# A gather that accumulates: keys and values added onto edge features and zeros in the attention stage of a graph network

## The chip, the cores and the metric

One Trainium2 chip, one of its cores. The metric is the device time of one execution in microseconds, median of three runs. An engine is TensorE (PE, its weight loads PEld), VectorE (DVE), ScalarE (ACT), GpSimd (POOL) or SyncE (SP); transfers run on 16 DMA engines.

## What is computed

2500 nodes with 256 features each, 40,000 edges sorted by destination. The program runs a relational graph layer, a mixture of six experts, an edge attention layer with a feed-forward part, and a mixture of eight experts. The change is in the attention:

```python
ep = ef @ We + be                                     # 40000 x 32, from 64 edge features
scores = einsum("ehd,ehd->eh", q[dst], k[src] + ep[:, None, :]) * scale
scores = scores * ew[:, None]
m = segment_max(scores, dst);  ex = exp(scores - m[dst]);  s = segment_sum(ex, dst)
out = segment_sum((ex / s[dst])[:, :, None] * v[src], dst)   # 8 heads of 32
```

Each edge needs the row of its source node in a table of keys and values (512 numbers, 2 KB), and the same 32 edge features are added to each of the 8 heads of the key.

## The kernel before, in words

The stages follow each other: loading, tables, sums and experts of the first half, then `stage_attention` (line 1749), whose first instructions run at 817 us of the profile. Behind it stand code paths for unsorted edges that don't run here.

`stage_attention` handles the edges in 79 groups of 4 tiles of 128 edges (TP = 4, NG = 79; 314 tiles in all, as the last group has two). Every engine has its own list of pieces, made by `order1` (line 1735) from two tables: SLOT1 says at which place of a slot a group's piece stands, so that piece `("add", -0.280)` of group 10 stands at 9.720, and BLOCK1 does the same for the ten blocks of 256 nodes of feed-forward and expert work that begin once their groups are done. Sorting by place gives the order in which an engine issues. The pieces of a group `i`:

- GpSimd gathers four times 128 rows of 2 KB from `table_kv` in HBM into the ring `kv` of 9 groups (line 1890, `att_kv<-table_kv,g_srcI`; RINGC = 9). Groups 0 to 2 wait for nothing, 3 to 8 for the add of three groups before, later ones until the sums of the group that had the place are done (`summed`, line 1887). After a group's first gather stands the join of an earlier group (line 1882), an accumulating DMA of 1 KB to `table_o`, whose waits hold up the three gathers behind it.
- SyncE loads the edge features (`eft`, line 2459, two buffers), the queries and selection matrices (lines 2452, 2453, 2470), and stores sums.
- TensorE makes the features in `psE` (line 2284, `features`, piece "feat") and the queries in `psQ` (line 2276), later sums weighted values (line 2301, `sums`).
- ScalarE copies `psE` to the buffer `epb`, 128 columns (line 2188, `features`), scales scores (line 2195), copies half of each sum (`odd`, line 2227).
- VectorE adds `epb` to the keys, each feature row repeated for 8 heads (line 1910, `add`), multiplies by the queries (line 1915), reduces to scores (line 1921), and 7 slots later multiplies the values by the weights (line 1997, `weigh`). A softmax over 4 groups at a time runs in between.

In the ring a tile has 8 spare columns, then 256 for keys and 256 for values. Semaphores tie the engines: `ep_made` (features in PSUM), `ep_ready` (in `epb`), `added`, `product`, `summed`.

## Time and profile before

| | us |
|---|---|
| three runs | 1721.68, 1724.7, 1732.46 |
| median of the runs | 1724.7 |
| span of the profiled execution, first to last instruction | 1668.6 |
| first gather of the attention stage issued | 817.55 |
| last one issued | 1485.6 |

No device time of its own is given for the profiled execution; the span lies 56.1 us below the median of the runs. Busy over the span: TensorE 1495.7 us (90%), VectorE 1028.6 (62%), ScalarE 615.6 (37%), GpSimd 781.2 (47%). The stage's end is what is late: the table of stretches tells which engine is full where. TensorE's clock has two levels, 1.2 and 2.4 GHz; the granted clock is given as a share of the higher one, so a stretch at 0.5 ran at the lower level, one at 0.6 mostly so.

### The profile page before, as it was taken

Reading aid. Unit: us, or ns where it says so; the run is one execution under the profiler, and the core shown is the slowest. Engines: PE = TensorE matmul, PEld = TensorE weight load, DVE = VectorE, ACT = ScalarE, POOL = GpSimd, SP = SyncE. Lnnn points to the kernel's source line nnn. Section 1 sums busy time; section 2 is a strip of 40 time slices with the busy share of each in tenths; the row PEclk is TensorE's granted clock in tenths of the full one; section 3 lists DMA queues with packets and bytes.
Section 4 is the critical chain, followed back from the end, with each engine's and each line's share of the span. In section 5 each row is a group of like instructions: output and inputs, shape, how many; then the busy total and the mean of one; then the engine's idle time right before and its main releaser. Section 6 shows DMA issues by size and latency. Waiting matters only on the chain. (4 is left out here: it accounts for less than half of the span.)

```text
span 1668.6 us, 23723 instructions
## 1 busy us (share of the span) xinstructions
PE 1495.7 (90%) x6795; PEld 1005.9 (60%) x6795; DVE 1028.6 (62%) x2542; ACT 615.6 (37%) x1534; POOL 781.2 (47%) x738
## 2 busy tenths in 40 slices
PE   4999788999999999998356799999999999999996
PEld 2554314665666777777233467767766767767785
DVE  6543244345445555545388789898898888896432
ACT  3121002333234343443022355554555445555341
POOL 1100277646755777600378666574746556540000
PEclk9999857999999999999556699999999999999997
DMA  8448456546766566631487885665757565641100
GB/s 258 164 161 261 142 151 172 154 115 191 213 175 180 166 190 178 164 94 47 137 252 216 267 253 165 193 180 167 208 152 212 143 196 169 179 122 39 29 7 9
DMA packets 191573, 270.07 MB, mean 162 GB/s; under 512 B 28295, under 2 KB 156035, under 8 KB 188867
## 3 DMA queue, kind: packets, MB, share of 16 engines
q1 hardware_dynamic: 148419, 144.77, 27.7%
q0 software_dynamic: 43008, 123.61, 26.8%
q8 instruction: 60, 0.98, 0.2%
q14 instruction: 86, 0.70, 0.1%
HBM read 196.22 MB, written 72.06 MB: 161 GB/s over the span
## 5 line engine op out<-in xcount | busy, mean ns | idle before, releaser
L1890 POOL DMA_INDIRECT att_kv<-table_kv,g_srcI x314 | 368.5, 1174 | 246.4 <-issue 180.4
L1149 POOL DMA_INDIRECT ex_hg<-table_h,z_idx x314 | 316.7, 1008 | 150.2 <-issue 84.9
L2441 PE MATMUL att_psR<-g_mw,att_h 128*128 128x256 f32 x640 | 163.9, 403 | 1.0 <-ACT att_h L2259 1.0
L2414 PE MATMUL att_psR<-att_t,g_mw 128*128 128x256 f32 (+1 forms) x640 | 154.8, 387 | 0.1
L1466 PE MATMUL ex_psG<-ex_hg,ex_oh 128*42 128x256 f32 x628 | 134.6, 427 | 13.3 <-DMA ex_hg<-table_h,z_idx 7.2
L751 PE MATMUL tab_psH<-e_u,tab_xT 128*128 128x512 f32 x320 | 142.6, 598 | 4.3 <-DVE e_u L532 4.3
L2441 PEld LDWEIGHTS att_psR<-g_mw,att_h 128*128 128x128 f32 x640 | 124.7, 200 | 23.0 <-ACT att_h L2259 4.0
L1387 ACT ACTIVATE ex_h<-ex_psH,g_cols 128x256 f32<-128x256 f32 (+1 forms) x240 | 97.3, 464 | 93.8 <-PE ex_psH L1488 93.1
L2414 PEld LDWEIGHTS att_psR<-att_t,g_mw 128*128 128x128 f32 x640 | 121.2, 199 | 16.6 <-issue 2.6
L1882 POOL DMA_DIRECT2D table_o<-att_part x59 | 54.2, 919 | 161.9 <-DMA table_o<-att_part 90.5
L2301 PE MATMUL att_psG<-att_kv,att_oh 128*42 128x264 f32 x628 | 109.5, 431 | 13.7 <-DVE att_kv L1997 13.3
L1910 DVE TENSOR_TENSOR att_kv<-att_kv,att_epb 128x1024 f32<-128x1024 f32 x79 | 96.4, 1220 | 39.9 <-DMA att_kv<-table_kv,g_srcI 32.9
L1501 PE MATMUL ex_psC<-e_experts,ex_h 128*128 128x256 f32 x480 | 114.0, 384 | 0.0
L1488 PE MATMUL ex_psH<-ex_xT,e_experts 128*128 128x256 f32 (+1 forms) x480 | 113.8, 380 | 0.1
L1215 DVE TENSOR_TENSOR ex_part<-ex_psG,ex_odd 42x256 f32<-42x256 f32 x79 | 32.5, 411 | 130.6 <-ACT ex_odd L1400 130.4
L1488 PE MATMUL ex_psH<-ex_h,e_experts 128*128 128x256 f32 (+1 forms) x480 | 111.6, 377 | 0.0
L2259 ACT ACTIVATE att_h<-att_psR,g_cols 128x256 f32<-128x256 f32 (+1 forms) x160 | 66.2, 464 | 116.8 <-PE att_psR L2414 116.4
L2105 DVE SCALAR_TENSOR_TENSOR att_acc<-att_psR,att_gate,att_acc 128x256 f32<-128x256 f32 x160 | 69.5, 475 | 59.8 <-PE att_psR L2441 59.8
L751 PEld LDWEIGHTS tab_psH<-e_u,tab_xT 128*128 128x128 f32 x320 | 60.8, 192 | 74.3 <-issue 71.0
L1501 PEld LDWEIGHTS ex_psC<-e_experts,ex_h 128*128 128x128 f32 x480 | 88.9, 190 | 19.6 <-issue 7.2
L1997 DVE TENSOR_TENSOR att_kv<-att_kv,att_p 128x1024 f32<-128x1024 f32 x79 | 95.5, 1209 | 7.0 <-ACT att_p L2212 6.9
L1488 PEld LDWEIGHTS ex_psH<-ex_xT,e_experts 128*128 128x128 f32 x480 | 87.7, 190 | 17.6 <-issue 7.7
(308 smaller groups left out, 2465.1 us busy)
## 6 DMA issues: line engine op xcount, KB each, us to landing
table_h<-tab_hs SPq DMA_DIRECT2D x20, 1024.0 KB, 4.0
att_eft<-in_eft SPq DMA_DIRECT2D x158, 64.0 KB
ex_db<-table_dst SPq DMA_DIRECT2D x79, 126.0 KB
table_ohT<-ex_ohT SPq DMA_DIRECT2D x79, 126.0 KB
att_ohT<-table_ohT SPq DMA_DIRECT2D x79, 126.0 KB
table_oh<-ex_oh SPq DMA_DIRECT2D x79, 84.0 KB, 2.3
att_oh<-table_oh SPq DMA_DIRECT2D x79, 84.0 KB, 4.0
table_kv<-ex_qkv SPq DMA_DIRECT2D x10, 512.0 KB, 4.8
```

Of the source, the lines that this page charges most:

```text
L751: ins = nc.tensor.matmul(psH[:, c % 4, :], xT[:, b % 2, k, q * P:(q + 1) * P], Wr[:, k, j * 512:(j + 1) * 512], start=(k == 0), stop=(k == ...
L1149: nc.gpsimd.indirect_dma_start(hg[:, t % RING0, :], None, d.h[:, :], bass.IndirectOffsetOnAxis(ap=g.idx0[:, t:t + 1], axis=0)).then_inc(go ...
L1387: nc.scalar.activation((h1 if what == "A" else h2)[:, e % 2, o, 0:used(b)], psH[:, n % 3, o * BLK0:o * BLK0 + used(b)], ACT.Relu, bias=vec ...
L1466: ins = nc.tensor.matmul(psG[at:at + WG, 0:D], oh[:, i % 3, t % TP, :], hg[:, t % RING0, :], start=(t <= second), stop=(t >= tiles(i)[-1] ...
L1488: ins = nc.tensor.matmul(psH[:, n % 3, o * BLK0:o * BLK0 + w_], w[:, e, k, o * P:(o + 1) * P], x[:, k, 0:w_], start=(k == 0), stop=(k == D ...
L1501: ins = nc.tensor.matmul(psC[:, e % 2 * BT0 + q, :], h2[:, e % 2, k, q * P:(q + 1) * P], g.w3[:, e, k, :], start=(k == 0), stop=(k == DK - 1))
L1890: nc.gpsimd.indirect_dma_start(kv[:, t % (RINGC * TP), H:H + 2 * D], None, d.kv[:, :], bass.IndirectOffsetOnAxis(ap=g.srcI[:, t:t + 1], ax ...
L1910: nc.vector.tensor_tensor(k, k, epb[:, i % 2, :, :].unsqueeze(2).to_broadcast([P, TP, H, DH]), ALU.add).then_inc(s.added, 1)
L1997: nc.vector.tensor_tensor(kv[:, b:b + TP, 0:H * VW].rearrange("p t (a c) -> p t a c", c=VW)[:, :, :, 0:DH], kv[:, b:b + TP, H + D:H + 2 * ...
L2301: ins = nc.tensor.matmul(psG[at:at + WG, 0:H * VW], oh[:, i % 3, t % TP, :], kv[:, t % (RINGC * TP), 0:H * VW], start=(t <= second), stop= ...
L2414: ins = nc.tensor.matmul(out[:, c * CB:c * CB + used(b)], g.mw1[:, e, k, c * P:(c + 1) * P], t3[:, k, 0:used(b)], start=(k == 0), stop=(k ...
L2441: ins = nc.tensor.matmul(out[:, q * D:(q + 1) * D], h1[:, n % 3, k, q * P:(q + 1) * P], g.mw2[:, e, k, :], start=(k == 0), stop=(k == DK - 1))
```

## The change

The buffer `epb` and VectorE's add are gone. ScalarE now writes into the ring before the gather comes: zeros into the 256 value columns of the four tiles, and the features, repeated for 8 heads, into the 256 key columns (`fill`, two copies of 128x1024). The gather is issued with `compute_op=ALU.add`, so that the DMA adds each row to what lies there. GpSimd waits for both copies of a group before its first gather; the ring's wait for `summed` has moved into `fill`, and groups 3 to 8 wait for `product` of three groups before. Features run further ahead: TensorE makes those of group `b + 3` at place 0.600 of slot `b` in place of group `b + 1` at -0.236, SyncE loads them up to group `b + 4`, and ScalarE fills group `b + 2` at -0.100. Features of a group stand tile by tile in `psE` by another output pattern.

```diff
 SLOT1 = {
-    "PE": (("sums", -0.271), ("feat", -0.236), ("cols", -0.027), ...
+    "PE": (("sums", -0.271), ("cols", -0.027), ... ("turnR", 0.580), ("feat", 0.600), ...
...
-                        if i >= RINGC and t % TP == 0:
-                            pool.wait_ge(s.summed, i - RINGC + 1)
-                        elif i >= 3 and t % TP == 0:
-                            pool.wait_ge(s.added, i - 2)
+                        if t % TP == 0:
+                            pool.wait_ge(s.keys_filled, i + 1)
+                            pool.wait_ge(s.values_cleared, i + 1)
+                            if 3 <= i < RINGC:
+                                pool.wait_ge(s.product, i - 2)
                         nc.gpsimd.indirect_dma_start(kv[:, t % (RINGC * TP), H:H + 2 * D], None, d.kv[:, :],
-                                                     bass.IndirectOffsetOnAxis(ap=g.srcI[:, t:t + 1], axis=0)).then_inc(kv_got[i % RINGC], 16)
+                                                     bass.IndirectOffsetOnAxis(ap=g.srcI[:, t:t + 1], axis=0), compute_op=ALU.add).then_inc(kv_got[i % RINGC], 16)
...
-                def add(i):
+                def multiply(i):
                     dve.wait_ge(kv_got[i % RINGC], 64 * (i // RINGC) + 16 * len(tiles(i)))
-                    dve.wait_ge(s.ep_ready, i + 1)
-                    k = keys(i).rearrange("p t (a c) -> p t a c", c=DH)
-                    nc.vector.tensor_tensor(k, k, epb[:, i % 2, :, :].unsqueeze(2).to_broadcast([P, TP, H, DH]), ALU.add).then_inc(s.added, 1)
-
-                def multiply(i):
-                    dve.wait_ge(s.added, i + 1)
                     dve.wait_ge(s.q_ready, i + 1)
                     nc.vector.tensor_tensor(keys(i), keys(i), psQ[:, :, :], ALU.mult).then_inc(s.product, 1)
...
-                def features(i):
+                def fill(i):
+                    b = i % RINGC * TP
+                    if i >= RINGC:
+                        act.wait_ge(s.summed, i - RINGC + 1)
+                    if i == 0:
+                        act.wait_ge(s.zero_made, 1)
+                    nc.scalar.copy(kv[:, b:b + TP, H + D:H + 2 * D], zero[:, 0:1].unsqueeze(2).to_broadcast([P, TP, D])).then_inc(s.values_cleared, 1)
                     act.wait_ge(s.ep_made, i + 1)
-                    if i >= 2:
-                        act.wait_ge(s.added, i - 1)
-                    nc.scalar.copy(epb[:, i % 2, :, :].rearrange("p (a t) c -> p t a c", a=2),
-                                   psE[:, 0:P].rearrange("p (t a c) -> p t a c", a=2, c=DH)).then_inc(s.ep_ready, 1)
+                    nc.scalar.copy(kv[:, b:b + TP, H:H + D].rearrange("p t (a c) -> p t a c", c=DH),
+                                   psE[:, 0:P].rearrange("p (t c) -> p t c", c=DH).unsqueeze(2).to_broadcast([P, TP, H, DH])).then_inc(s.keys_filled, 1)
...
-                        features(0)
+                        fill(0)
+                        fill(1)
...
-                        queries(0)
-                        features(0)
+                        for i in range(3):
+                            features(i)
+                        queries(0)
...
+                        load_features(2, features)
+                        load_features(3, features)
```

In the changed kernel the multiply is line 1910, the reduction 1916, the gather 1891, ScalarE's two copies 2182 (zeros) and 2184 (features), the copy of half a sum 2224, the scaling of scores 2191, TensorE's features 2280 and queries 2271.

VectorE, one slot early in the stage, before (1997 is `weigh`, 2009 the sum of two halves):

```order
L1910 TENSOR_TENSOR att_kv<-att_kv,att_epb 128x4x256
L2009 TENSOR_TENSOR att_part<-att_psG,att_odd 42x264
L1997 TENSOR_TENSOR att_kv<-att_kv,att_p 128x4x8x32
L1915 TENSOR_TENSOR att_kv<-att_kv,att_psQ 128x4x256
L1921 TENSOR_REDUCE att_S<-att_kv 128x32
```

and now:

```order
L2004 TENSOR_TENSOR att_part<-att_psG,att_odd 42x264
L1992 TENSOR_TENSOR att_kv<-att_kv,att_p 128x4x8x32
L1910 TENSOR_TENSOR att_kv<-att_kv,att_psQ 128x4x256
L1916 TENSOR_REDUCE att_S<-att_kv 128x32
L2004 TENSOR_TENSOR att_part<-att_psG,att_odd 42x264
```

The row of the add is gone, the others follow as they did, with the multiply directly behind `weigh`.

ScalarE, the same place of the program, before (2219 copies the softmax weights beside the values):

```order
L2227 COPY att_odd<-att_psG 42x264
L2219 COPY att_kv<-att_p 128x4x8
L2188 COPY att_epb<-att_psE 128x2x2x32
L2195 ACTIVATE att_S<-att_S,g_ews 128x8 x4
L2227 COPY att_odd<-att_psG 42x264
```

and now:

```order
L2224 COPY att_odd<-att_psG 42x264
L2182 COPY att_kv<-att_zero 128x4x256
L2184 COPY att_kv<-att_psE 128x4x256
L2216 COPY att_kv<-att_p 128x4x8
L2191 ACTIVATE att_S<-att_S,g_ews 128x8 x4
```

One copy of 128 columns, behind the weights, has become two of 1024, in front of them and behind `odd`.

SyncE at the start of the stage, behind the features, selection and queries of group 0 and the features of group 1, before:

```order
L2452 DMA att_ohT<-table_ohT 126x512
L2453 ISA
L2453 DMA att_qw<-table_q 126x256
L2465 DMA att_mk<-table_masks 128x386 x2
L2470 DMA att_oh<-table_oh 128x168 x3
L2459 DMA att_eft<-in_eft 64x256 x2
```

and now:

```order
L2447 DMA att_ohT<-table_ohT 126x512
L2448 ISA
L2448 DMA att_qw<-table_q 126x256
L2454 DMA att_eft<-in_eft 64x256 x4
L2460 DMA att_mk<-table_masks 128x386 x2
L2465 DMA att_oh<-table_oh 128x168 x3
```

Two more groups of features are loaded ahead of the masks and windows.

## Rows read from the trace of the kernel before

**Rows 1.** Which engines are busy in which stretch: busy us (instructions), granted clock, DMA share

```profile
817.00:860.00 43.00, 16.57 (x67) 11.90 (x68) 24.43 (x32) 7.41 (x29) 33.00 (x32) 0.50 0.87 257
...
1500.00:1668.60 168.60, 144.20 (x682) 117.32 (x680) 70.67 (x212) 61.14 (x122) 3.90 (x5) 0.93 0.07 21
817.00:960.00 143.00, 86.90 (x344) 49.06 (x346) 107.78 (x156) 37.43 (x143) 108.03 (x95) 0.59 0.83 245
960.00:1500.00 540.00, 520.18 (x2743) 379.79 (x2740) 470.67 (x950) 273.87 (x735) 310.73 (x274) 0.98 0.63 181
```

**Rows 2.** The page, chain that ended last, by engine

```profile
PE 27%; DVE 8%; issue 5%; POOL 4%; DMA 3%; ACT 1%; SPq 1%; POOLq 0%; DVEq 0%
```

**Rows 3.** TensorE's waits, 960 to 1500 us: waiting, releaser, total us, times, longest

```profile
PE att_psR L2428 <- DVE att_gate L967: 8.5, 7, 1.3
PE att_psR L2433 <- ACT att_gateT L2266: 3.8, 7, 0.5
PE att_psT L2340 <- DVE att_fnew L1951: 2.5, 5, 0.8
PE att_psE L2284 <- ACT att_epb L2188: 2.1, 6, 0.4
PE att_psR L2314 <- DVE att_n L2025: 1.7, 1, 1.7
```

**Rows 4.** Waits of all engines, 817 to 960 us

```profile
DVE att_kv L1910 <- DMA att_kv<-table_kv,g_srcI: 17.4, 10, 2.7
```

**Rows 5.** DMA queues and one issue row, 817 to 960 us: packets, MB, share

```profile
q0 software_dynamic: 6957, 21.90, 51.7%
q1 hardware_dynamic: 16732, 12.95, 30.3%
...
att_kv<-table_kv,g_srcI POOLq DMA_INDIRECT x86, 4.6
```

**Rows 6.** DMA queues, 960 to 1500 us

```profile
q0 software_dynamic: 19891, 60.50, 39.7%
q1 hardware_dynamic: 47496, 36.42, 22.9%
```

**Rows 7.** The page, costliest groups: busy us, mean ns of one, idle before

```profile
L1882 POOL DMA_DIRECT2D table_o<-att_part x59 | 54.2, 919 | 161.9 <-DMA table_o<-att_part 90.5
...
L1910 DVE TENSOR_TENSOR att_kv<-att_kv,att_epb 128x1024 f32<-128x1024 f32 x79 | 96.4, 1220 | 39.9 <-DMA att_kv<-table_kv,g_srcI 32.9
```

**Rows 8.** Timeline of the stage's start: start us, us, engine, line

```profile
817.55 1.08 POOL L1890 DMA_INDIRECT att_kv<-table_kv,g_srcI  x1 [93.13 <-issue]
818.27 1.16 SPq L2459 DMA_DIRECT2D att_eft<-in_eft  x2
...
820.65 0.36 SPq L2453 DMA_DIRECT2D att_qw<-table_q  x1
...
822.72 0.95 POOL L1890 DMA_INDIRECT att_kv<-table_kv,g_srcI  x1 [0.30 <-issue]
...
825.32 1.01 PE L2276 MATMUL att_psQ<-att_qw,att_ohT 126*128 126x256 bf16 x4 [18.42 <-DMA att_qw<-table_q]
...
826.12 0.95 PE L2284 MATMUL att_psE<-g_we,att_eft 128*128 128x64 f32 x4
...
828.77 1.22 DVE L1915 TENSOR_TENSOR att_kv<-att_kv,att_psQ 128x1024 f32<-128x1024 f32 x1
```

**Rows 9.** The reduction of line 1921, one per group, 860 to 960 us

```profile
860.00:960.00 100.00, 16.60 (x15) 0.63 0.81 240
```

**Rows 10.** DMA queues around one 1 MB store, 68.8 to 74.5 us

```profile
q1 hardware_dynamic: 144, 1.05, 44.5%
```

**Rows 11.** ScalarE's groups by shape, 817 to 1500 us

```profile
L2188 ACT COPY att_epb<-att_psE 128x128 f32<-128x128 f32 x79 | 20.7, 262 | 39.3 <-PE att_psE L2284 38.7
...
L2254 ACT COPY att_t<-att_psR 128x512 f32<-128x512 f32 x7 | 4.1, 586 | 6.5 <-PE att_psR L2314 6.5
```

**Rows 12.** Timeline, one expert layer's matmuls

```profile
1207.31 1.89 PE L2414 MATMUL att_psR<-att_t,g_mw 128*128 128x256 f32 x8
```

More of the change, by code:

```diff
@@ L2109, in program @@
                     if not redo:
+                        nc.vector.memset(zero[:, :], 0.0).then_inc(s.zero_made, 1)
                         nc.vector.memset(ends[:, :, :], -FAR)
@@ L2231, in program @@
                                 scale(i)
-                        if what == "feat":
-                            i, j = b, b - LAG
-                            if i + 1 < NG:
-                                features(i + 1)
+                        if what == "fill" and b + 2 < NG:
+                            fill(b + 2)
                         if what == "att":
@@ L2345, in program @@
                                 queries(i + 1)
[L2346 to L2349 removed]
+                        if what == "feat" and b + 3 < NG:
+                            features(b + 3)
                         if what == "ends":
@@ L2513, in steps @@
                                     load_windows(j + 3)
-                        if what == "loadE" and b + INS < NG:
-                            load_features(b + INS, features)
+                        if what == "loadE" and b + 4 < NG:
+                            load_features(b + 4, features)
                         if what == "loadQ" and b + INS < NG:
```

25 lines of the change are left out of this document (9 added, 16 removed).

## The prediction

> **What bounds the kernel now.** I read the view by stretches first. The attention stage (817 to 1668.6 us) falls into three parts [rows 1]. From 817 to 960 us the matmul engine is busy 87 of 143 us at a granted clock of 0.59, so it is mostly at the 1.2 GHz level and not the limit; VectorE is busy 108 us, GpSimd 108 us and the DMA engines 83%. Three resources are close to each other there. From 960 to 1500 us TensorE is busy 520 of 540 us at clock 0.98: it is the bound, VectorE has 69 us free, DMA is at 63%. From 1500 us no gather is left, DMA is at 7%, and the rest is expert matmuls.
>
> The chain that ended last agrees: TensorE has 27% of the span in it, VectorE 8%, GpSimd's gather 4%, DMA 3% [rows 2]. The waits say what TensorE lacks in the middle part: its five named waits make 18.6 us in 540, of which 12.7 us are for VectorE (8.5, 2.5 and 1.7) [rows 3]. In the first part VectorE's add waited for the gather ten times, 17.4 us in all [rows 4]: gathers already arrive late there.
>
> Last, the DMA queues. q0, the queue that GpSimd feeds, carries practically only this gather. It took 51.7% of the 16 engines' time from 817 to 960 us, q1, all that SyncE issues, 30.3% [rows 5]; from 960 to 1500 us 39.7% and 22.9% [rows 6]. So one gather of 256 KB costs the engines 73.9 us / 86 = 0.86 us in the first part, and over the stage (73.9 + 214.4) / 314 = 0.92 us.
>
> **The change part by part.**
>
> *The add.* 79 instructions of 1220 ns, 96.4 us of VectorE [rows 7]. About 20 of them lie before 960 us (86 gathers at 4 a group [rows 5], which lead the add by one or two groups), 24 us. The other 59 (72 us) lie beside TensorE's matmuls; at most the 12.7 us that TensorE waited for VectorE can come back. In the first part at most 24 us can, and only if gathers keep up. They hardly can: a group is 4 gathers of 0.95 us [rows 8] and a join of 0.92 us [rows 7], each with 0.30 us before it, so 4 × 1.25 + 1.22 = 6.22 us of GpSimd, against a pace of 100 us / 15 groups = 6.67 us [rows 9]. Over the 20 groups that caps the gain at 20 × 0.45 = 9 us. What is late next is the gather itself.
>
> *The add inside the gather.* The sum now needs the destination's old 256 KB beside the source's: 82 MB more to read from SBUF. No row shows a large accumulating transfer (the joins move 1 KB), so I bound it. From below: the second read is hidden and costs nothing, 0.92 us stays. From above: it costs as much again as the gather, 1.84 us. The nearest row of a read out of SBUF is a 1 MB store of the tables stage: 44.5% of 5.7 us is 2.54 us of engine time for 1.05 MB, 2.42 us per MB [rows 10]. I take that, put behind the gather's own time, since it is the only measured price of that leg: 0.262 MB × 2.42 = 0.63 us more, 1.55 us a gather, 1.69 times as much.
>
> First part: 73.9 + 21.9 MB × 2.42 (53.0) + 43.3 for q1 = 170.2 us of engine time for what took 143 us. The highest mean share that the stretches show is 0.87, while engines still waited for other things [rows 1]; pressed harder I take 0.90. 170.2 / 0.90 = 189 us: **+46 us**. VectorE's 24 us lie within these waits, so they give nothing.
>
> Middle part: 214.4 + 60.5 MB × 2.42 (146.4) + 123.7 = 484.5 us, 0.90 of 540. That is just at the edge, **0 us**; at 0.87 it would be 557, +17. The at most 12.7 us of TensorE's waits for VectorE go into the waits for gathers.
>
> *The order of the start.* Before, the first gather was issued at 817.55 us, beside the loads, and the first multiply began at 828.77 [rows 8]. Now the gather must wait for features: eft's load (issued 818.27 to 819.43), landing some 4.6 us later as qw's did (820.65 to 825.3), 0.95 us of features matmul, 1.0 us of ScalarE copy, four gathers of 1.25 us, a landing of 4.6 us [rows 5]: 819.4 + 4.6 + 0.95 + 1.0 + 5 + 4.6 = 835.6, seven late. Later groups are fed by the same queues that are the limit of this part, so it is not caught up, save for perhaps 1 us of idle time before the third group: **+6 us**.
>
> *ScalarE's two copies.* From its copies of 128x128 (262 ns) and 128x512 (586 ns) [rows 11] a column costs 0.84 ns, so 1024 columns take 1.02 us. Two of them replace one of 262 ns: +1.78 us a group, 79 groups, 140 us. ScalarE was busy 274 of 540 us in the middle part and goes to 379 [rows 1], behind which nothing is queued that TensorE lacks at once: expert layers are issued two ahead, and one layer's matmuls take 1.9 us [rows 12], nearly as long as both copies. I cost it at nothing; without that cover a copy pair would hold TensorE perhaps 1 us in 59 groups, 59 us.
>
> *The rest.* The gather's wait moves from `summed` to a fill that itself waits for `summed`, so group i is issued some 2 us later than before, and used 0.6 of a slot later (multiply in place of add, 0.6 × 8.5 us): even. Behind GpSimd's wait stands the join, for which SyncE's next wide store waits at every fourth group. TensorE's features matmuls keep their count and only move. SyncE's two feature loads go three groups ahead, no bytes added. The memset of `zero` is one of 128x1. All 0; if features came late they would now hold a gather, not an add, and the ring of two feature buffers is unchanged, so I allow 5 us for it.
>
> Sum: 46 + 0 + 6 = +52 us on the profiled execution. Its span is 1668.6 us; the median of the three runs is 1724.7, so 56 us lie around the span, untouched. 1724.7 + 52 = **1777 us**. With the share at 0.87 the same sum gives 1724.7 + 53 + 17 + 6 = 1801.
>
> **The rivals.**
>
> *R1, the second read costs as much as the first* (1.84 us a gather). First part 147.8 + 43.3 = 191.1, at 0.90 212 us, +69; middle 428.8 + 123.7 = 552.5, at 0.90 614 us, +74; start +6: 1874 us. At a share of 1.0 it would be 48 + 13 + 6, 1792. For it: both reads pass the same engines, which show no spare rate above 0.9. Against: SBUF reads went at 2.42 us per MB, not 3.5. The Trainium skill, "Collectives: The Full Stack", section "The bandwidth ceiling: the fold count and why AG ≠ RS ≠ AR", says that an add in the DMA path costs nothing by itself but needs two source reads on one ring, so it runs at about half the rate of a copy; by its ratio of 1.93 the sum would lie just under R1. No large accumulate in this trace confirms it.
>
> *R2, both legs run at the store's rate* (2 × 0.63 = 1.27 us, as if part of the gather's time were waiting that the second leg fills). First part 2 × 53.0 + 43.3 = 149.3, at 0.90 166 us, +23; middle 2 × 146.4 + 123.7 = 416.5 of 540, no bound; start +6, minus half of the 12.7 us of waits: 1748 us. For it: the store shows that the engines can pass 413 GB/s (1 / 2.42), where the gather reaches 21.9 MB / 73.9 us = 296. Against: no row shows that one read fills the other's waiting.
>
> *R3, the other side: the second read is hidden.* The DMA share stays as it is and VectorE's time comes back: −9 in the first part (GpSimd's floor), −13 in the middle, +6 for the start: 1709 us. If GpSimd's gathers also shorten, and the start is caught up, all of −24 − 13: 1688. It decides as soon as an accumulating gather costs under about 1.0 us of engine time: then 86 × 1.0 + 43.3 = 129 us still fit into 143 at 0.90. For it: GpSimd's join, which accumulates too, is no dearer to issue than a plain gather [rows 7, 8]. Against: two reads must be paid somewhere.
>
> *R4, the change takes the work from VectorE but puts it in TensorE's way through ScalarE*, 59 us as above with a free accumulate: 1709 + 59 = 1768. Against: TensorE waited for ScalarE 5.9 us in 540 [rows 3].
>
> **How the numbers follow.** Forecast 0.35, R1 0.17, R2 0.15, R3 0.28, R4 0.05. R1 spreads from 1792 to 1874 and R3 from 1688 to about 1720; the range leaves out the outer end of each, a tenth of the chance on either side: 1705 to 1860. What a measurement of this kernel tells from no change is about 1%, 17 us, so the bounds are 1707 and 1742. Slower: the forecast but for 0.01, R1, R4 and 0.08 of R2, 0.64. Within 1%: 0.11 of R3 (1709 lies 2 us inside), 0.07 of R2 and that 0.01, 0.19. Faster: the better part of R3, 0.17.
>
> **What would show it.** Right: q0's share per gather rises to about 1.55 us of engine time; the DMA share from 817 to 960 us at 0.9; multiply waits for the gather in nearly every early group; the last gather is issued some 50 us later than 1485; the stretch after the last gather is unchanged. VectorE loses 96 us of busy time and gains as much idle. The start is read from the first multiply, 7 us later. ScalarE's copies at 1.0 us each. Wrong: q0 per gather at or under 1.0 us (R3), at 1.84 us (R1), GpSimd's own instruction grown well beyond 0.95 us (a cost that I put at nothing: each 0.25 us of it adds 1 us a group where GpSimd is at its floor), or TensorE idle behind ScalarE (R4).

## The result, and the profile after

On the chip that timed the change, the kernel before takes 1723.7 us (median of 4 runs, 1721.7 to 1732.5) and the changed one 1777.1 us (4 runs, 1773.3 to 1779.0): ratio 1.0324, 95% interval 1.0274 to 1.0373, 53 us slower. The forecast said 1777.0. The number was met by luck. The sections below show that its account was met only in part: one term was sized about right for a mostly wrong reason, one was missing, and on other chips the same change costs 77 us and not 53.

The first thing to read is the span. The profiled execution of after took 1776.4 us with a span of 1774.6, so less than 2 us lie around the span, not 56. The profile of before [rows 1] has a span of 1668.6 us, and the kernel before took 1666 to 1670 us (medians) on the three chips of most experiments below; it took 1723.7 us where the change was timed, and 1722.8 on the chip of c13. So "span against median" compared two chips. I call the chip that timed the change the timing chip. In after's profile the unchanged stages ahead of the attention end at 856 us and not at 817.

**The stage by stretches.** After: the first 144 us, the middle, and what follows the last gather (columns: window, its length, busy us and instructions of TensorE, its loads, VectorE, ScalarE, GpSimd, granted clock, DMA share, GB/s).

```profile
856.00:1000.00 144.00, 69.75 (x269) 38.26 (x269) 65.75 (x98) 58.45 (x132) 117.35 (x77) 0.50 0.99 190
1000.00:1500.00 500.00, 447.35 (x2291) 325.74 (x2291) 349.12 (x768) 315.77 (x671) 376.33 (x242) 0.94 0.93 176
1596.00:1774.60 178.60, 154.21 (x741) 123.61 (x739) 80.19 (x229) 66.82 (x137) 7.20 (x8) 0.94 0.10 25
```

Against [rows 1]: in the first stretch the DMA engines are at 0.99 where they were at 0.83, GpSimd is busy 117 us for 77 instructions where it needed 108 for 95, and TensorE and VectorE do far less. In the middle TensorE is busy 89% of the time, not 96%, and its granted clock is 0.94, not 0.98; that window of after still holds some of the early groups. The stretch after the last gather is no longer than before (178.6 us; from 1485.6 to 1668.6 it was 183).

**The gather.** Page of after, costliest groups (busy us, mean ns of one, idle before and what ended it), and the two DMA queues from 857 to 1600 us:

```profile
L1891 POOL DMA_INDIRECT att_kv<-table_kv,g_srcI x314 | 523.6, 1667 | 243.2 <-ACT att_kv L2184 153.9
...
L1910 DVE TENSOR_TENSOR att_kv<-att_kv,att_psQ 128x1024 f32<-128x1024 f32 x79 | 95.7, 1211 | 74.3 <-DMA att_kv<-table_kv,g_srcI 71.5
...
L1992 DVE TENSOR_TENSOR att_kv<-att_kv,att_p 128x1024 f32<-128x1024 f32 x79 | 95.7, 1211 | 48.3 <-ACT att_p L2209 47.0
...
L1882 POOL DMA_DIRECT2D table_o<-att_part x59 | 75.5, 1280 | 80.3 <-DMA table_o<-att_part 58.3
```

```profile
q0 software_dynamic: 46809, 82.27, 70.5%
q1 hardware_dynamic: 63872, 49.12, 23.1%
```

q0 took 0.705 of 743 us for 314 gathers, 1.67 us of engine time each; it was 0.92 [rows 5, 6], so 1.82 times as much. It makes 149 packets a gather, where before it made 85 (26848 packets for 314 [rows 5, 6]). The instruction on GpSimd grew as well, from typically 0.95 us [rows 8] (median 974 ns) to 1.54 (median 1543), and the join from 919 ns [rows 7] to 1280. The mean of a gather lies higher in both kernels, 1667 ns here and 1174 in the page of before:

```profile
L1890 POOL DMA_INDIRECT att_kv<-table_kv,g_srcI x314 | 368.5, 1174 | 246.4 <-issue 180.4
```

The forecast had GpSimd's room from the 0.95 us. VectorE no longer has the add (96.4 us) and waits for gathers 71.5 us instead of 32.9. The wait of line 1992 is new in size: VectorE waits 47.0 us for the exponentials that ScalarE makes.

**ScalarE and the chain.** ScalarE's two fills by shape, and the chain that ended last:

```profile
L2182 ACT COPY att_kv<-att_zero 128x1024 f32<-128x1024 f32 x79 | 82.3, 1041 | 10.4 <-DVE att_zero L2105 10.4
L2184 ACT COPY att_kv<-att_psE 128x1024 f32<-128x1024 f32 x79 | 79.9, 1012 | 11.8 <-PE att_psE L2280 10.0
```

```profile
PE 21%; ACT 9%; DVE 6%; issue 5%; POOL 5%; DMA 4%; SPq 1%; POOLq 0%; DVEq 0%
```

A fill takes 1.0 us, as worked out. ScalarE had 1% of the chain [rows 2] and has 9%.

**The start.** Timeline of after (start us, us, engine, line; in brackets the idle time before and what ended it):

```profile
856.07 1.16 SPq L2454 DMA_DIRECT2D att_eft<-in_eft  x2
...
858.95 1.09 PE L2280 MATMUL att_psE<-g_we,att_eft 128*128 128x64 f32 x4 [14.26 <-DMA att_eft<-in_eft]
...
860.08 1.01 ACT L2184 COPY att_kv<-att_psE 128x1024 f32<-128x1024 f32 x1 [0.95 <-PE att_psE L2280]
861.36 1.64 POOL L1891 DMA_INDIRECT att_kv<-table_kv,g_srcI  x1 [99.20 <-ACT att_kv L2184]
...
863.30 1.56 POOL L1891 DMA_INDIRECT att_kv<-table_kv,g_srcI  x1 [0.30 <-issue]
...
874.19 1.22 DVE L1910 TENSOR_TENSOR att_kv<-att_kv,att_psQ 128x1024 f32<-128x1024 f32 x1 [15.43 <-DMA att_kv<-table_kv,g_srcI]
```

Features, fill, first gather, and four gathers before the first multiply can start: 18.1 us from the load to the multiply. The kernel before needed 10.5 [rows 8], and 12.6 in its second profile (c1).

### The profile page after: what moved, and what is told of

Its sections match the earlier page's. It is cut to its first block, busy times and chain, and to the rows that moved or that the text cites. A ratio compares the mean times of both kernels' runs of the same rounds, so it can differ in the third digit from the quotient of the medians.

```text
span 1774.6 us, 23647 instructions
## 1 busy us (share of the span) xinstructions
PE 1513.0 (85%) x6795; PEld 1017.4 (57%) x6795; DVE 943.9 (53%) x2464; ACT 747.6 (42%) x1613; POOL 931.5 (52%) x738
## 4 chain that ended last, share of the span: by engine, by line
PE 21%; ACT 9%; DVE 6%; issue 5%; POOL 5%; DMA 4%; SPq 1%; POOLq 0%; DVEq 0%
PE att_psR L2436 7%; POOL att_kv L1891 4%; PE att_psR L2409 3%; PE att_psR L2385 3%; PE att_psG L2297 2%; PE att_psR L2394 2%; ACT att_kv L2184 2%; ACT att_kv L2182 2%; DVE att_kv L1910 2%; ACT L2254 2%; DMA table_o<-att_part 1%; ACT att_h L2254 1%; DMA att_kv<-table_kv,g_srcI 1%; DMA att_eft<-in_eft 1%; ACT L2207 1%
## 5 line engine op out<-in xcount | busy, mean ns | idle before, releaser
L1891 POOL DMA_INDIRECT att_kv<-table_kv,g_srcI x314 | 523.6, 1667 | 243.2 <-ACT att_kv L2184 153.9
L2436 PE MATMUL att_psR<-g_mw,att_h 128*128 128x256 f32 x640 | 167.6, 409 | 11.2 <-ACT att_h L2254 11.2
L1910 DVE TENSOR_TENSOR att_kv<-att_kv,att_psQ 128x1024 f32<-128x1024 f32 x79 | 95.7, 1211 | 74.3 <-DMA att_kv<-table_kv,g_srcI 71.5
L1992 DVE TENSOR_TENSOR att_kv<-att_kv,att_p 128x1024 f32<-128x1024 f32 x79 | 95.7, 1211 | 48.3 <-ACT att_p L2209 47.0
L1882 POOL DMA_DIRECT2D table_o<-att_part x59 | 75.5, 1280 | 80.3 <-DMA table_o<-att_part 58.3
L1400 ACT COPY ex_odd<-ex_psG 42x256 f32<-42x256 f32 x79 | 29.1, 368 | 199.5 <-PE ex_psG L1466 102.9
L2254 ACT ACTIVATE att_h<-att_psR,g_cols 128x256 f32<-128x256 f32 (+1 forms) x160 | 66.0, 463 | 102.0 <-PE att_psR L2409 100.8
L1466 PEld LDWEIGHTS ex_psG<-ex_hg,ex_oh 128*42 128x42 f32 x628 | 43.8, 126 | 104.0 <-issue 86.3
```

The lines of the kernel that those rows point to most:

```text
L1466: ins = nc.tensor.matmul(psG[at:at + WG, 0:D], oh[:, i % 3, t % TP, :], hg[:, t % RING0, :], start=(t <= second), stop=(t >= tiles(i)[-1] ...
L1891: nc.gpsimd.indirect_dma_start(kv[:, t % (RINGC * TP), H:H + 2 * D], None, d.kv[:, :], bass.IndirectOffsetOnAxis(ap=g.srcI[:, t:t + 1], ax ...
L1910: nc.vector.tensor_tensor(keys(i), keys(i), psQ[:, :, :], ALU.mult).then_inc(s.product, 1)
L2254: nc.scalar.activation(h1[:, n % 3, k, 0:used(b)], psR[:, bank["A", b, e], k * CB:k * CB + used(b)], ACT.Gelu, bias=vec(g, "mb1", 2 * e + ...
L2436: ins = nc.tensor.matmul(out[:, q * D:(q + 1) * D], h1[:, n % 3, k, q * P:(q + 1) * P], g.mw2[:, e, k, :], start=(k == 0), stop=(k == DK - 1))
```

## The experiments

Each was run beside the kernel before on the same chip, and the ratio is to that. They ran in four sets, each on a chip of its own: c1 to c4 (before: 1667.9 us), c5 to c8 (1669.7), c9, c10 and c12 (1666.3), and c13 on a chip where before takes 1722.8. Beside the times stands what separated the theories best: when VectorE's reduction, one per group, starts for the 1st, 21st, 31st, 71st and 79th time in each profile's timeline, and what is left of the span then. In after these reductions stand at 875.45 and, for example,

```profile
1141.16 1.21 DVE L1916 TENSOR_REDUCE att_S<-att_kv 128x32 f32<-128x1024 f32 x1
...
1536.67 1.21 DVE L1916 TENSOR_REDUCE att_S<-att_kv 128x32 f32<-128x1024 f32 x1
```

for the 31st and the 71st group: 40 groups in 395.5 us.

| kernel | median us | ratio (95%) | 1st starts at | 1 to 21 | 21 to 31 | 31 to 71 | 71 to 79 | rest |
|---|---|---|---|---|---|---|---|---|
| before | 1668 | 1 | 830.0 | 136.6 | 92.0 | 372.9 | 73.4 | 163.7 |
| c1 before, once more | 1665.5 | 1.000 (0.997 to 1.003) | 834.5 | 132.7 | 91.2 | 372.1 | 73.4 | 163.8 |
| c6 plain gather, narrow fills | 1654.6 | 0.992 (0.989 to 0.995) | 833.0 | 125.2 | 93.0 | 363.3 | 72.8 | 163.8 |
| c12 the same, ScalarE kept busy | 1685.4 | 1.012 (1.009 to 1.015) | 830.0 | 130.3 | 97.2 | 388.3 | 73.7 | 163.7 |
| c2 plain gather, wide fills | 1701.2 | 1.020 (1.014 to 1.025) | 831.8 | 133.3 | 98.4 | 395.5 | 76.0 | 163.9 |
| c3 c2 and GpSimd work | 1719.3 | 1.032 (1.027 to 1.037) | 830.7 | 149.8 | 97.0 | 395.6 | 75.9 | 162.0 |
| c7 c2 and DMA traffic | 1730.5 | 1.037 (1.033 to 1.041) | 832.5 | 155.3 | 105.9 | 395.4 | 76.0 | 163.4 |
| c8 every second accumulates | 1716.7 | 1.029 (1.025 to 1.033) | 833.5 | 148.0 | 97.6 | 395.4 | 75.9 | 163.5 |
| c4 accumulates 1 KB rows | 1734.4 | 1.042 (1.036 to 1.047) | 834.0 | 164.1 | 96.9 | 395.5 | 76.0 | 162.0 |
| c9 accumulates, narrow fills | 1710.3 | 1.027 (1.023 to 1.031) | 836.0 | 170.2 | 95.9 | 365.2 | 71.1 | 164.0 |
| c10 fills behind the weights | 1756.6 | 1.053 (1.049 to 1.056) | 840.4 | 168.8 | 103.5 | 405.6 | 74.8 | 163.7 |
| c5 the changed kernel | 1746.6 | 1.047 (1.043 to 1.050) | 835.7 | 171.7 | 100.3 | 395.5 | 76.0 | 165.2 |
| after: the changed kernel, timing chip | 1777.1 | 1.032 (1.027 to 1.037) | 875.5 | 168.4 | 97.3 | 395.5 | 75.9 | 162.0 |
| c13 zeros by VectorE | 1769.4 | 1.028 (1.024 to 1.032) | 873.5 | 169.2 | 100.8 | 385.9 | 72.7 | 163.7 |

One profile stands behind each row. Two profiles of the same kernel show how far a column can be trusted: before and c1 differ by 4.4 us at the start, 3.9 in groups 1 to 21 and at most 0.9 in the others; c5 and after by 3.3, 3.0 and 3.2 us in groups 1 to 21, 21 to 31 and the rest, and by 0.1 or less in 31 to 71 and 71 to 79.

Two columns carry the finding. "1 to 21" follows the gather (c2, c3, c8, c4 and c5 have the same ScalarE), and "31 to 71" does not: it is 395.5 us with any gather as long as ScalarE's fills are wide, and 363 to 365 with narrow ones, whether the gather accumulates or not.

### c1: the kernel before, once more

> The kernel before, profiled once more. The two profiles differ before the attention stage too: its first gather goes out at 817 us in the profile of before and its first feature load at 856 us in that of the changed kernel, in code that the change does not touch. Theory A (the profile of before caught a shorter execution than its timed ones): this profile has a span near 1720 us and a first gather 30 to 50 us later than 817. Rival (the early stages really run faster before): span near 1670 again, first gather near 817, and the timed runs have 50 us outside the span.

1665.5 us (10 runs), ratio 0.9998 (0.9969 to 1.0027); its profiled execution took 1669.0 us with a span of 1667.5. Theory A falls: the span is near 1670 again, as its rival had it, with the first gather at 819.9 us. But nothing large lies around the span either. The 56 us were a difference between two chips (or two occasions; no run separates these).

### c2: the changed kernel with a plain gather

```diff
-  bass.IndirectOffsetOnAxis(ap=g.srcI[:, t:t + 1], axis=0), compute_op=ALU.add)
+  bass.IndirectOffsetOnAxis(ap=g.srcI[:, t:t + 1], axis=0))
```

The gather overwrites the features, so they are not added: this part of the computation is left out.

> The changed kernel with the accumulate taken out of the gather and all else kept (ScalarE's two copies, the waits, the order; the keys then lack the edge features). If the accumulate is what costs (my step 2), the time falls to that of before or somewhat under it: 1705 to 1735 us, a gather at 0.95 us on GpSimd and 0.9 us of DMA engine time. If ScalarE's copies or the later start cost (R4, step 3), it stays over 1750 us.

1701.2 us: 33 us over the kernel before with no accumulate at all and no add on VectorE. The bounds of c2 to c4 were written for a chip where before takes 1723.7 us; taken as differences, c2 should have come out between 19 us faster and 11 slower if only the accumulate cost. 33 slower is past the 26 from which it was to be ScalarE's copies or the later start. It falls in no term of the forecast. Page of c2:

```profile
PE 26%; ACT 12%; DVE 8%; issue 3%; DMA 2%; POOL 1%; SPq 0%; DVEq 0%; POOLq 0%
...
L1891 POOL DMA_INDIRECT att_kv<-table_kv,g_srcI x314 | 325.9, 1038 | 386.7 <-ACT att_kv L2184 306.5
...
L1992 DVE TENSOR_TENSOR att_kv<-att_kv,att_p 128x1024 f32<-128x1024 f32 x79 | 95.7, 1211 | 51.3 <-ACT att_p L2209 51.3
```

The gathers are early (GpSimd waits for ScalarE, 306.5 us), and ScalarE has 12% of the chain. The wait of line 1992 for the exponentials was 6.9 us in the kernel before.

### c3: GpSimd's time alone

```diff
+  if t > 0:
+      pool.wait_ge(s.idled, t)
+  nc.gpsimd.memset(idle[:, :], 0.0).then_inc(s.idled, 1)
```

behind each plain gather, a memset of 128x512. Here, too, the features are not added.

> The plain gather again, with a memset of 128x512 on GpSimd behind each gather, which puts back about the 0.6 us by which the accumulating gather is longer on GpSimd (1.54 in place of 0.95 us), with no added DMA traffic. Theory G (GpSimd's time to issue is the new bound: 4 x 1.84 + 1.6 = 9.0 us a group): at least two thirds of the loss comes back, 1755 to 1785 us. Theory D (the DMA engines' doubled reads are the bound, my forecast): under 1740 us.

1719.3 us, 18 us over c2. GpSimd's timeline:

```profile
859.18 0.95 POOL L1893 DMA_INDIRECT att_kv<-table_kv,g_srcI  x1 [0.17 <-issue]
860.14 0.54 POOL L1897 MEMSET att_idle<- 128x512 f32 x1
860.84 0.95 POOL L1893 DMA_INDIRECT att_kv<-table_kv,g_srcI  x1 [0.17 <-issue]
```

A gather with its memset takes 1.66 us, a group 6.64. From the 1st to the 11th reduction, where joins have hardly begun, a group took 6.76 us. GpSimd's time alone sets the pace there. But c3 gives less than the accumulate's issue: a plain gather with its gap is 0.95 + 0.30 = 1.25 us, this pair 1.66, the accumulating one 1.54 + 0.30 = 1.84. It put back 0.41 us of 0.59, as the gap shrank to 0.17, so its 18 us are only a part of what GpSimd's longer instruction costs. The two thirds that theory G wanted, 30 of 45 us, did not come back; by this run alone neither theory holds.

### c4: accumulate, half the bytes

```diff
-  nc.gpsimd.indirect_dma_start(kv[:, t % (RINGC * TP), H:H + 2 * D], None, d.kv[:, :],
+  nc.gpsimd.indirect_dma_start(kv[:, t % (RINGC * TP), H:H + D], None, d.x2[:, :],
```

Rows of 1 KB from another table are added onto the keys; neither keys nor values of the source node are gathered.

> The changed kernel with half as many bytes in each accumulating gather: 1 KB rows of another table of as many rows, added onto the keys only; the values stay zero. GpSimd's instruction and count stay. Theory G: the instruction stays at about 1.54 us and the time within 15 us of 1777. Theory D: DMA engine time per gather falls to 0.55 of 1.67 us, and the time to 1725 us or below.

1734.4 us, 12 under c5 and 33 over c2: theory G was right in both its signs. The instruction is as long as with 2 KB rows (median 1544 ns). The window from 860 to 910 us lies in the first ten groups of both kernels; c4, then c5:

```profile
860.00:910.00 50.00, 24.74 (x104) 13.81 (x105) 28.91 (x48) 19.94 (x49) 42.40 (x28) 0.53 0.67 120
```

```profile
860.00:910.00 50.00, 26.23 (x108) 14.96 (x108) 27.73 (x46) 21.67 (x53) 42.23 (x28) 0.53 1.02 189
```

The engines' share is 0.67 and 1.02, GpSimd's busy time the same (42 us and 28 gaps of 0.30 us fill the 50), and the first ten groups took the same, 75.8 and 76.0 us. So there the length of GpSimd's instruction is the limit, not the engines. From the 11th to the 21st, c4 takes 88.2 us and c5 95.7: there the larger transfers add 7.5 us.

The same reading for all of groups 1 to 21, in before, c2, c4 and c5:

```profile
830.03:966.59 136.56, 90.26 (x368) 50.73 (x369) 109.99 (x158) 39.46 (x150) 103.96 (x90) 0.62 0.84 250
```

```profile
831.76:965.10 133.34, 88.54 (x364) 49.40 (x366) 87.50 (x138) 71.32 (x168) 96.02 (x92) 0.58 0.87 259
```

```profile
833.96:998.05 164.09, 89.95 (x364) 50.38 (x366) 88.08 (x138) 71.09 (x167) 139.85 (x89) 0.55 0.73 142
```

```profile
835.67:1007.34 171.67, 92.74 (x374) 52.03 (x374) 88.00 (x137) 72.66 (x170) 137.42 (x90) 0.56 1.01 197
```

With 0.30 us before each instruction GpSimd fills 131 of 137 us in the kernel before, 124 of 133 in c2, all 164 in c4 and 164 of 172 in c5. GpSimd was full in this part before the change already, at a mean gather of nearly 1.2 us, so what its instruction grows by can't hide there: from c2 to c5 its busy time grows by 41 us and the stretch by 38. c4 pays 31 of these 38 with the DMA engines at 0.73.

### c5: the changed kernel on this chip

> The changed kernel itself, as the anchor of the other runs on this chip, where the kernel before takes 1668 us and not 1723. Theory P (the change costs the same share everywhere, as it lies in the attention stage alone, and that stage is as long on both chips): the attention stage was 851 us before and 918 after, +67 us, so 1735 us, ratio 1.040; about 17 of the 56 us that the faster chip saves were saved in the stages ahead. Rival C (the change costs 3.24% wherever it runs): 1722 us.

1746.6 us, ratio 1.0465, 77 us slower. Rival C, the same 3.24% on every chip, falls (1722 us), and theory P (1735) came 12 us short. The changed kernel's attention stage is not longer on the timing chip (918.5 us there, 928 here), so it would have to be the kernel before that is slower in this stage there; no profile of it on that chip was taken.

### c6: narrow fills

```diff
-  nc.scalar.copy(kv[:, b:b + TP, H + D:H + 2 * D], zero[:, 0:1].unsqueeze(2).to_broadcast([P, TP, D]))
+  nc.scalar.copy(kv[:, b:b + TP, H + D:H + D + 8], zero[:, 0:1].unsqueeze(2).to_broadcast([P, TP, 8]))
...
-  nc.scalar.copy(kv[:, b:b + TP, H:H + D].rearrange("p t (a c) -> p t a c", c=DH),
-                 psE[:, 0:P].rearrange("p (t c) -> p t c", c=DH).unsqueeze(2).to_broadcast([P, TP, H, DH]))
+  nc.scalar.copy(kv[:, b:b + TP, H:H + DH], psE[:, 0:P].rearrange("p (t c) -> p t c", c=DH))
```

on top of c2.

> Plain gather, with the order, the waits and the late start of the change, but ScalarE writes only 8 columns of zeros and 32 columns of features a tile (two copies of 128x32 and 128x128, some 0.5 us together in place of 2.05). The features are not added: this leaves part of the computation out. With wide copies the plain gather took 1701 us, 33 over the kernel before. Theory S (ScalarE's 2.05 us a group, in front of the exponentials, the weights and half of each sum, is what costs these 33 us): at or under the kernel before, 1640 to 1665 us, VectorE's wait for the softmax weights gone (51 us with wide copies), and the difference from 1701 is the price of the width. Rival O (the late start and GpSimd's and TensorE's new waits cost it): above 1680 us. If VectorE's add was worth something, it shows here: 7 for the start is lost and up to 22 won.

1654.6 us, 47 us under c2: the width of the two copies costs more than everything else in c2. It also shows what losing VectorE's add is worth while the copies are small: 15 us. Of that 7 to 11 came in groups 1 to 21, by which profile of before one takes, and 9 to 10 in 31 to 71.

TensorE's waits from 1100 to 1500 us (total us, times, longest), c6, then c5:

```profile
PE att_psR L2422 <- DVE att_gate L967: 7.9, 6, 1.3
PE att_psR L2427 <- ACT att_gateT L2260: 3.3, 6, 0.5
```

```profile
PE att_psR L2436 <- ACT att_h L2254: 8.6, 5, 1.7
PE att_psR L2423 <- DVE att_gate L967: 6.6, 5, 1.3
PE att_psR L2428 <- ACT att_gateT L2261: 4.4, 5, 0.9
PE att_psG L2296 <- DVE att_crow L1985: 3.6, 11, 0.3
PE att_psG L2297 <- issue: 3.1, 6, 0.5
PE att_psE L2280 <- ACT att_kv L2184: 3.0, 5, 0.6
PE att_psT L2328 <- ACT att_S L2191: 2.8, 5, 0.6
```

11.2 us in 400 became 32.1, of which 18.8 are for ScalarE. The largest one is new: the second matmuls of an expert layer wait for the activation that ScalarE makes. No single wait is large; ScalarE is late for the experts, the scores and the features by turns, and for VectorE's exponentials.

The waits are not all of it. Groups 31 to 71, c6 and then c2:

```profile
1051.28:1414.58 363.30, 352.87 (x1896) 262.13 (x1895) 280.99 (x622) 195.59 (x547) 191.27 (x191) 1.00 0.64 184
```

```profile
1063.46:1458.98 395.52, 363.60 (x1896) 267.52 (x1895) 280.54 (x621) 256.13 (x546) 191.61 (x191) 0.97 0.59 169
```

Of the 32.2 us between them TensorE is idle for 21.5; in the other 10.7 it is busy, with the same 1896 matmuls, at a granted clock of 0.97 in place of 1.00. A third of what the wide fills cost here is slower matmuls.

### c7: DMA traffic alone

```diff
+  sp.dma_start(d.scratch[b * P:(b + 1) * P, :], g.f1[:, :, :].rearrange("p k c -> p (k c)")).then_inc(s.extra, 16)
```

in SyncE's program once a group, 1 MB each, on top of c2.

> Plain gather with wide fills, and SyncE stores 1 MB from SBUF to a scratch table once a group, so that the DMA engines have the reads of the old contents to do (some 2.5 us of engine time a group, as 4 x 0.63 were forecast), while GpSimd's instructions stay at 0.95 us. Features are not added: part of the computation is left out. Theory D (the engines' second read is what the accumulate costs): DMA share near 1 in the first part and near 0.9 in the middle, and 1725 to 1745 us, as the changed kernel. Theory G (GpSimd's instruction, 1.54 us in place of 0.95, is what costs; the engines had the room): 1701 to 1712 us, with VectorE's wait for the gather little above that of the plain one. The loads of SyncE stand behind the stores, which can make queries late: this would show as TensorE's wait for them and not for the gather.

1730.5 us, 29 over c2: the time that theory D named. But it can't be read as the price of the accumulate's traffic, since the edge features stand behind these stores in SyncE's queue: TensorE waited 55.0 us for them, where it waited 22.3 in c2, and VectorE's wait for the gather did not grow (20.7 us, 20.5 in c2), which is what theory G said. The run decides nothing between them.

### c8: every second gather accumulates

```diff
-  compute_op=ALU.add)
+  **(dict(compute_op=ALU.add) if t % 2 else {}))
```

> Gathers of odd tiles accumulate, those of even tiles are plain; all else is the changed kernel. Features are not added to even tiles: part of the computation is left out. GpSimd needs 2 x 1.84 + 2 x 1.25 + 1.6 = 7.8 us a group instead of 8.95 or 6.6; the engines 4 x (0.92 + 1.67) / 2 = 5.2 us a group for q0 instead of 6.7 or 3.7. Plain was 1701, the changed kernel about 1735. Theory L (each accumulate costs its share): halfway, 1718. Theory K (a resource that only binds past its edge, engines at 1.0 in the first part): nearer to plain, 1703 to 1710.

1716.7 us. Half the accumulates cost 15.6 us of the 45.4 that all of them cost (c5 less c2), a third. The expectation took 1735 for the whole; with the 1746.6 measured, halfway would be 1724. So the price is not in proportion throughout. By stretches: in the first ten groups c2, c8 and c5 take 56.8, 66.0 and 76.0 us, which is half the price for half the accumulates, as a limit by GpSimd's instruction gives; in the next ten 76.5, 82.0 and 95.7, less than a third of it.

### c9: accumulate with narrow fills

The fills of c6 from the tenth group on, and the gather of the change.

> The accumulating gather with narrow fills: full fills for the first nine groups, as the ring starts unwritten, and from then on 8 columns of zeros and 32 of features a tile, so that the gather adds onto what lies there and the output is left wrong in values. It prices the accumulate without ScalarE's load. On this chip: plain with narrow fills 1655, plain with wide fills 1701 (+46), accumulate with wide fills 1747 (+46 more). Theory I (the two costs are in different parts of the stage and add: the accumulate costs in the first part, where GpSimd is full, the wide fills in the rest): 1655 + 46 = 1701. Theory H (in the middle part ScalarE's delay now hides the accumulate; without it the pace would be 11.3 groups in 100 us, for which GpSimd needs 11.3 x (4 x 1.84 + 1.6) = 101 us and the engines 0.75 + 0.25 = 1.0, so the gather itself is the limit all through): 1710 to 1730, and VectorE waits for gathers after 1000 us, too.

1710.3 us, 56 over c6, at the lower edge of theory H. But the reason given for H is wrong: the profile's middle has no wait of VectorE for a gather from 1100 us on, and shows

```profile
1100.00:1500.00 400.00, 387.21 (x2075) 288.92 (x2074) 309.96 (x695) 213.32 (x589) 314.50 (x208) 0.99 0.97 183
```

TensorE is busy 97% at clock 0.99 with the engines at 0.97: groups 31 to 71 take 365.2 us beside 363.3 in c6. The accumulate costs 2 us there. Its price lies in groups 1 to 21, 45.0 us, with 3 each for the start and the next ten groups. (The first nine fills of c9 are wide; in the first ten groups wide fills cost 4 us between c6 and c2, so up to 4 of the 45 are theirs.)

### c10: the fills behind the weights

```diff
-  "ACT": (("odd", -0.123), ("fill", -0.100), ("exp", 0.044), ("pw", 0.245), ("scale", 1.507)),
+  "ACT": (("odd", -0.123), ("exp", 0.044), ("pw", 0.245), ("fill", 0.300), ("scale", 1.507)),
```

> The changed kernel with one number changed: ScalarE's fill stands at 0.300 of its slot, behind the exponentials and the copy of the weights, and no longer in front of them at -0.100. It computes all. Theory R (it is the place: 2.05 us in front of the exponentials hold up VectorE's weighing and TensorE's sums, 51 us of VectorE's waits): most of the 46 us comes back, 1700 to 1715, and VectorE's wait for the softmax weights falls from 47 to under 15 us. Theory T (it is the load: wherever they stand, two copies of 1 us delay something that TensorE waits for, its scores or its expert layers): 1735 to 1747, with the waits moved to the scores, half sums or expert activations.

1756.6 us, 10 slower than the change. Waits from 817 to 1600 us:

```profile
PE att_psQ L2271 <- DVE att_kv L1910: 30.4, 10, 6.4
PE att_psE L2280 <- ACT att_kv L2184: 27.8, 13, 2.9
```

VectorE's wait for the exponentials fell to 17.0 us, as theory R said, and the time did not follow: that wait was not what cost. TensorE's features now wait 27.8 us for the fill, and VectorE waits 100.1 us for gathers (73.5 in c5). Theory R falls; the waits moved as theory T said, though the time lies over its range too.

### c12: ScalarE busy, nobody waits for it

```diff
+  if i > 0:
+      act.wait_ge(s.spared, 2 * i)
+  for n in range(2):
+      nc.scalar.copy(spare[:, n, :], zero[:, 0:1].to_broadcast([P, 740])).then_inc(s.spared, 1)
```

behind the narrow fills of c6.

> Plain gather and narrow fills, and behind each pair of them ScalarE makes two copies of 740 columns (about 0.81 us each) to a buffer that nothing reads, so that ScalarE is as long at this place as with wide fills, while GpSimd and TensorE are released as early as with narrow ones. Features are not added: part of the computation is left out. Theory S (what costs is that ScalarE comes late to its next pieces): as with wide fills, 1695 to 1705. Theory W (what costs is that the gather and TensorE's next features are released late): as with narrow fills, 1655 to 1665.

1685.4 us, between both theories: 31 of the 46.6 us between c6 and c2 come from ScalarE being occupied, though nothing waits for these copies. The other 16 go with the wide fills themselves, which release GpSimd and TensorE later; that this is why they cost was not shown. (The two copies together with the narrow fills are 2.10 us a group, as long as the wide fills.)

### c13: the zeros by VectorE

```diff
+  def clear(i):
+      b = i % RINGC * TP
+      if i >= RINGC:
+          dve.wait_ge(s.summed, i - RINGC + 1)
+      nc.vector.memset(kv[:, b:b + TP, H + D:H + 2 * D], 0.0).then_inc(s.values_cleared, 1)
```

as a piece of VectorE at -0.150, in place of ScalarE's copy of line 2182.

> The changed kernel with the zeros written by VectorE (a memset of 128x1024 at place -0.150, the wait for the ring's sums moved with it) and only the features by ScalarE. It computes all. VectorE's memset of 128x256 takes 0.27 us, so one of 128x1024 takes 1.0 to 1.1 us, less than the add it lost (1.22); ScalarE is rid of 79 x 1.04 us. Theory L (each us of ScalarE in a group costs alike; the wide fills' extra 1.57 us cost 46 us, or 29 us of the total for each us): 1747 - 30 = 1717 us if VectorE has the room, and the pace in the middle part rises from 10.4 to about 11 groups in 100 us. Rival V (the time that VectorE won is spent again and delays multiply and weigh as the add did): 1730 to 1745. Neither is as fast as the kernel before, 1668, as the gather's doubled work in the first part stays.

1769.4 us where before takes 1722.8, ratio 1.0279. The change itself had 1.0324 beside the same time of before. In the stretch from 1140 to 1540 us, the change and then c13:

```profile
1140.00:1540.00 400.00, 366.48 (x1912) 269.81 (x1911) 283.51 (x623) 259.31 (x551) 302.43 (x194) 0.97 0.91 169
```

```profile
1140.00:1540.00 400.00, 377.59 (x1971) 280.49 (x1969) 324.59 (x692) 229.14 (x524) 316.14 (x199) 0.97 0.93 174
```

ScalarE is relieved, TensorE does more, and groups 31 to 71 need 385.9 instead of 395.5 us. The first part stays as it was, and the whole gain, about 8 us, is within the uncertainty of the two ratios. Theory L promised 30 us and falls; a gain of 8 is in the range that rival V gave (2 to 17 us under the change), and TensorE's waits in groups 31 to 71 of c13 bear V out:

```profile
PE att_psR L2429 <- DVE att_gate L967: 8.1, 5, 1.6
PE att_psG L2302 <- DVE att_crow L1991: 5.8, 3, 2.2
...
PE att_psR L2434 <- ACT att_gateT L2267: 2.7, 5, 0.5
```

In after TensorE waited in the same groups 18.8 us for ScalarE and 9.9 for VectorE; here it is 2.7 and 14: part of what one engine gave back the other took.

None of these beats the kernel before, except c6, which is the change without its purpose.

## Why the forecast came out, step by step

The parts can be read off the table, on chips where before takes 1668 us: c5 less before is 75.7 us of span, made of 5.7 at the start, 35.1 in groups 1 to 21, 8.3 in 21 to 31, 22.6 in 31 to 71, 2.6 to the last group and 1.5 after it. (Against c1 in place of before, the first two are 1.2 and 39.0.) The forecast had 6, 46, and 0 for the rest. By cause, the 77 us between the medians are 46.6 for the wide fills and 45.4 for the accumulate on top of them, less the 15 that c6 gains; the forecast had 0, 46 with 6 for the start, and 0.

**The start: the order right, the size within the spread.** Seven us late were forecast and +6 booked. From the first load to the first multiply the changed kernel takes 18.1 us (after; 18.0 in c5), the kernel before 10.5 and 12.6 (c1): 5.5 to 7.6 us more. What the stage loses by it is less certain, as the first reduction of c5 begins 5.7 us later than in before and 1.2 later than in c1.

**The add: right.** It was said to be worth at most 9 us at the start and 12.7 in the middle, if gathers kept up, which gave R3's 1709, a gain of 16. With the gather plain and the fills narrow (c6) the gain was 15, though GpSimd's floor, from which the 9 came, was taken with gathers of 0.95 us where their mean was nearly 1.2. In the changed kernel nothing of it is left, as forecast: VectorE's 96 us turned into waits, in after 39 us more for gathers and 40 more for the exponentials.

**The add inside the gather: the size near, the reason for the most part not.** The step priced engine time, 1.55 us a gather, and said that the engines at 0.90 would cost 46 us in the first part. Engine time is 1.67 us, between that and R1's 1.84, and the engines went to 1.0 and not 0.90. The two errors offset each other: by the same sum, 86 × 1.67 + 43.3 at a share of 1.0 is 187 us, +44. But the limit of the first part is another one, which was put at nothing: GpSimd's instruction, which grew by 0.59 us on an engine that was full already. c4 has that growth with half the bytes and keeps 33 of the 45 us that the accumulate costs (c5 over c2); c3, with 0.41 us of it and no accumulate, costs 18. The larger transfers make up the other 12 us, most of it behind the eleventh group. The forecast's own list of what would show it wrong named this growth, "a cost that I put at nothing". Its arithmetic there (0.25 us of it is 1 us a group) comes near what the chip did: 4 × 0.59 = 2.4 us a group for 20 groups is 47 us, against 38 measured between c2 and c5. The Trainium skill, "Collectives: The Full Stack", section "The bandwidth ceiling: the fold count and why AG ≠ RS ≠ AR", says of two collectives that the one with an add needs two source reads and runs at about half the rate of the one that copies, measured at a ratio of 1.93. The traces agree in size: these gathers took 1.82 times the engine time.

**The middle costs the gather nothing: right.** q0 and q1 were put at 0.90 of the engines, "just at the edge, 0 us": c9 less c6 is 2 us in groups 31 to 71.

**ScalarE's copies cost nothing: wrong.** This is the step that failed: "I cost it at nothing; without that cover a copy pair would hold TensorE perhaps 1 us in 59 groups, 59 us". The duration was right, 1.0 us a copy; the cover did not hold. Wide fills cost 46.6 us (c2 less c6), nearly the price that R4 put on them with a chance of 0.05. The argument against R4, that TensorE waited for ScalarE only 5.9 us in 540 [rows 3], looked at a ScalarE with 1.8 us less work in a group: a wait near zero says how late an engine is now, not how much later it may be. Two thirds of the price, 31 us, come with ScalarE being occupied, whatever it does (c12); the waits point to its pieces holding one another up (exponentials, scores, expert activations), and at a busy share of 65% in the middle TensorE waits 18.8 us in 400 for it. R4 had no term for the clock: a third of the price in groups 31 to 71 is matmuls at 0.97 of the clock instead of 1.00, in the run in which TensorE is idle three times as long. That the idle time brought the lower clock no run shows by itself. Three quarters of the fills' price lie behind the 31st group, where the accumulate costs 0 to 2 us.

**56 us around the span: wrong.** Under 2 us lie there. Harmless here, since the term was "untouched" in the sum, but it stood for a chip on which this kernel behaves otherwise.

So it is luck that 1777 was met. The forecast was 52 us of difference where the chips with a profile of both kernels show 77: it left out 46.6 us for the fills, and on the other side it left out the 15 that the add is worth and counted the start, 6 us, beside the accumulate, whose 45.4 contain it. 46.6 - 15 - 6 is the 25 us by which it is short. The timing chip happens to show 53. Why it is smaller there stays open: after's attention stage is 9 us shorter on the timing chip than in c5, and before's would be longer, by subtraction 1723.7 - 1.8 - 856 = 866 us against 851, if its stages ahead end at 856 us there as after's do; which stretch of it, no profile shows. The ratio of 1.047 is the one that the traces explain.

## What to carry to other kernels

Before moving work to an idle engine, look at what stands behind it in that engine's list, and not only at its busy share or at how long others wait for it now: ScalarE at half load had no room for 1.6 us a group, neither in front of its other pieces nor behind them (c10). Where a change has two costs, time a marker that comes once per unit of work in each variant and compare the stretches; equal times of the whole can hide two different limits. Read the clock beside the waits, since the matmuls themselves can have become slower. And before a span is set against a median, check that both are from the same chip.

## What the runs showed of the hardware

- An accumulating gather of 128 rows typically occupies GpSimd 1.54 us (after, c5), with rows of 1 KB (c4) as with rows of 2 KB, and a plain one of 2 KB rows 0.95 (medians 951 to 974 ns in before, c2 and c6); its engine time is 1.82 times the plain one's (1.67 against 0.92 us). The small accumulating join had been no dearer to issue than a plain gather (0.92 us in before), which R3 took as a point in its favour.
- The engines' share was 0.99 over 144 us in after and 1.01 over 172 us in c5, and in the middle of c9 it was 0.97 while TensorE worked 97% of the time; 0.87, the highest that before showed, was no ceiling.
- The same program takes 1668 us on some chips and 1723 on others. Ahead of the changed stage the profiles differ by 38 us (from 200 to 300 and from 400 to 500 us TensorE is busy 66 and 87 us in after's profile, 85 and 99 in before's), and this change cost 3.2% where before takes 1723.7 and 4.7% where it takes 1669.7.
- With the add gone, the gather's mean fell from 1174 to 1038 ns in c2, though its shortest stayed at 941. No run separated what had lengthened it.
